# Scores from opposite row halves, five score places and chunks weighed in twos in the last block of an attention

## The reference, cut to what matters

```python
c = jnp.concatenate([mem, kv], axis=1)                       # mem and kv are the same context
qh = (q @ w_q).reshape(B, L, N_HEAD, D_HEAD).transpose(0, 2, 1, 3)
kvp = c @ w_kv
k, v = (kvp[..., :D_HEAD], kvp[..., D_HEAD:])
attn_score = jnp.einsum('bhid,bjd->bhij', qh, k) / np.sqrt(D_HEAD)
attn_prob = jax.nn.softmax(attn_score, axis=-1)
out = jnp.einsum('bhij,bjd->bhid', attn_prob, v)
return out.transpose(0, 2, 1, 3).reshape(B, L, D) @ w_concat
```

## Time and profile before

| | |
|---|---|
| median of 3 runs | 2044.11 us |
| lowest, highest run | 2040.64, 2044.14 us |
| profiled execution, span from first to last instruction | 2039.6 us |
| of it, the last block, first score to copy of its sums | 1214.7 to 1285.3 us |
| mean granted TensorE clock | 0.986 of full |

### The profile page before, as it was taken

How to read it: one execution, slowest core, us unless ns; L and a number is a source line. 1 busy time by engine, 2 the same in 40 slices (tenths; PEclk the granted TensorE clock), 3 DMA queues, 4 the chain that set the end, 5 groups by cost and what they waited for, 6 DMA issues and landing times. The chain is left out here.

```text
span 2039.6 us, 36001 instructions
## 1 busy us (share of the span) xinstructions
PE 1959.2 (96%) x14245; PEld 969.3 (48%) x14245; DVE 1573.2 (77%) x2868; ACT 1355.8 (66%) x2394; POOL 100.9 (5%) x85
## 2 busy tenths in 40 slices
PE   7779999999999999999999999999999998999997
PEld 2225744444444444444444444444344444777755
DVE  7997899999999999999999981233688865444344
ACT  5333488888888888888888887432578874443321
POOL 1661000000000000000000000000200000000000
PEclk8999999999999999999999999999999999999999
DMA  4210000000000000000000000232000000000000
GB/s 148 73 62 0 1 2 2 2 1 2 1 1 2 2 1 2 2 2 1 1 2 1 2 2 1 60 120 65 0 1 1 2 1 0 1 1 1 16 29 28
DMA packets 25043, 32.66 MB, mean 16 GB/s; under 512 B 5967, under 2 KB 20335, under 8 KB 24622
## 3 DMA queue, kind: packets, MB, share of 16 engines
q1 hardware_dynamic: 23694, 28.30, 4.5%
q10 hardware_dynamic: 1184, 2.10, 0.3%
HBM read 29.61 MB, written 0.65 MB: 15 GB/s over the span
## 5 line engine op out<-in xcount | busy, mean ns | idle before, releaser
L1069 DVE TENSOR_REDUCE sb_max_partial<-ps_max_ps 128x1 f32<-128x512 f32 (+1 forms) x1664 | 977.3, 662 | 43.9 <-PE ps_max_ps L836 43.1
L1053 ACT ACTIVATE sb_probs<-ps_score_ps 128x512 f32<-128x512 f32 (+1 forms) x1632 | 875.1, 597 | 117.6 <-PE ps_score_ps L974 71.7
L974 PE MATMUL ps_score_ps<-sb_q_stack,sb_key_stack 64*128 64x512 f32 x1632 | 586.6, 443 | 3.9 <-ACT sb_probs L1053 3.4
L836 PE MATMUL ps_max_ps<-sb_key_stack,sb_q_stack 64*128 64x512 f32 (+1 forms) x1560 | 555.9, 438 | 0.0
L963 PE MATMUL ps_acc_ps<-sb_probs,sb_val_ones 128*32 128x256 f32 x6528 | 465.0, 387 | 0.0
L974 PEld LDWEIGHTS ps_score_ps<-sb_q_stack,sb_key_stack 64*128 64x128 f32 x1632 | 275.8, 183 | 321.5 <-ACT sb_probs L1053 257.2
L836 PEld LDWEIGHTS ps_max_ps<-sb_key_stack,sb_q_stack 64*128 64x128 f32 x1560 | 265.0, 184 | 9.8 <-DVE sb_max_partial L1069 7.5
L963 PEld LDWEIGHTS ps_acc_ps<-sb_probs,sb_val_ones 128*32 128x32 f32 x6528 | 156.3, 108 | 207.7 <-issue 140.5
L1721 DVE TENSOR_REDUCE sb_s_max_partial<-ps_s_ps 128x1 f32<-128x512 f32 x256 | 158.5, 682 | 24.6 <-PE ps_s_ps L1567 24.5
L1708 ACT ACTIVATE sb_s_probs<-ps_s_ps 128x512 f32<-128x512 f32 x256 | 140.8, 597 | 30.8 <-PE ps_s_ps L1595 22.8
L1942 DVE TENSOR_SCALAR_CACHE_REDUCE sb_x_scores<-ps_x_score_ps 128x1024 f32<-128x1024 f32 (+1 forms) x56 | 62.0, 1110 | 69.2 <-PE ps_x_score_ps L1929 69.2
(11 more groups left out here) (299 smaller groups left out, 1802.7 us busy)
## 6 DMA issues: line engine op xcount, KB each, us to landing
sb_val<-c_rows SPq DMA_DIRECT2D x16, 512.0 KB, 3.6
sb_e_gate_rows<-e_gate_dram SPq DMA_DIRECT2D x15, 512.0 KB, 3.9
sb_e_w<-L_ffn_rW SPq DMA_DIRECT2D x30, 128.0 KB, 2.1
sb_e_w<-L_ffn_W_T SPq DMA_DIRECT2D x24, 128.0 KB, 2.1
sb_ctx_T<-ctx_T SPq DMA_DIRECT2D x1, 1664.0 KB, 7.6
sb_ctx_T<-ctx_T ACTq DMA_DIRECT2D x1, 1538.0 KB, 8.6
sb_x_T<-x_T SPq DMA_DIRECT2D x1, 512.0 KB, 3.8
sb_x_tok<-x ACTq DMA_DIRECT2D x1, 512.0 KB, 11.0
```

The costliest lines, as they stand in the source:

```text
L836: nc.tensor.matmul(bank((blk, u))[:, 0:n], queries, keys, start=True, stop=True).then_inc(tile_ready, 1)
L974: nc.tensor.matmul(score_ps[:, e % 3, :], k.key_stack[rows(blk), c * P:(c + 1) * P], q_stack[rows(blk), blk // 2, j * HALF:(j + 1) * HALF] ...
L1053: nc.scalar.activation(probs[0:n, c % 3, j * HALF:(j + 1) * HALF], score_ps[0:n, e % 3, :], ACT.Exp).then_inc(exp_done, 1)
L1069: nc.vector.tensor_reduce(partial[:, blk % 2, h, r:r + 1], bank((blk, u))[:, 0:RANGES[r][1]], AX.X, ALU.max).then_inc(tile_used, 1)
```

## The change

Only the last block's order and places change, and one copy is added in block 1:

- The second score of each chunk (odd e) reads keys from rows 0 to 63 and queries from rows 0 to 63 of `q_first`, instead of rows 64 to 127 of the stacks. So the two scores of a chunk use opposite halves of the array's rows.
- For this, ACT copies the second half of block 15's queries (64 x 512) from `q_stack` to `q_first`, in block 1 behind chunk 12 (`lower_queries`). The shift rows of that half are later moved to `q_first` instead of `q_stack`.
- The last block's scores use five PSUM places: the three of `score_ps` and places 2 and 3 of `max_ps`. A score waits for the exponential five before it.
- Its chunks are weighed two at a time, after scores 7, 11, 15, ... 99, two and three chunks behind; chunks 48, 49 and 50 are weighed after the last score.

```diff
--- before.py
+++ after.py
@@ -777,7 +777,7 @@
 
 
 
-            TURN_AT, LAST_AT, FIRST_TURN = 28, NCH - 1, 66
+            TURN_AT, LAST_AT, FIRST_TURN, LOWERED_AT = 28, NCH - 1, 66, 12
             first = [(0, u) for u in range(FIRST_TURN + 1)] + [(0, "A")] + [(0, u) for u in range(FIRST_TURN + 1, TILES)]
 
 
@@ -858,7 +858,16 @@
                 eng.wait_ge(shift_turned, 2 * blk + (1 if half == "A" else 2))
                 lo = HALF_P * (blk % 2) + TERMS
                 cols = slice(0, HALF) if half == "A" else slice(HALF, BLK)
-                copy(q_stack[lo:lo + 2, blk // 2, cols], bank((blk, half))[0:2, :]).then_inc(shift_ready[half], 1)
+                if blk == NB - 1 and half == "B":
+                    to = q_first[TERMS:TERMS + 2, cols]
+                else:
+                    to = q_stack[lo:lo + 2, blk // 2, cols]
+                copy(to, bank((blk, half))[0:2, :]).then_inc(shift_ready[half], 1)
+
+            def lower_queries(act):
+
+                act.wait_ge(tile_used, TILES)
+                nc.scalar.copy(q_first[0:HALF_P, HALF:BLK], q_stack[rows(NB - 1), NT - 1, HALF:BLK].bitcast(F32))
 
             def q_bank(i):
 
@@ -964,16 +973,30 @@
                                            probs[:, v % 3, q * QUART:(q + 1) * QUART], start=(v == 0), stop=(v == NCH - 1))
                 ins.then_inc(pv_done, 1)
 
+            LAST_BANKS = 5
+
+            def score_bank(blk, e):
+                if blk < NB - 1:
+                    return score_ps[:, e % 3, :]
+                i = e % LAST_BANKS
+                return score_ps[:, i, :] if i < 3 else max_ps[:, i - 1, :]
+
             def score(pe, blk, e):
 
                 c, j = divmod(e, JOBS)
                 if c == 0:
                     pe.wait_ge(shift_ready["AB"[j]], blk + 1)
-                if not (blk == 0 and e < 3):
-                    pe.wait_ge(exp_done, blk * EXPS + e - 2)
-                nc.tensor.matmul(score_ps[:, e % 3, :], k.key_stack[rows(blk), c * P:(c + 1) * P],
-                                 q_stack[rows(blk), blk // 2, j * HALF:(j + 1) * HALF], start=True,
-                                 stop=True).then_inc(score_ready, 1)
+                if blk < NB - 1 or e < 3:
+                    if not (blk == 0 and e < 3):
+                        pe.wait_ge(exp_done, blk * EXPS + e - 2)
+                elif e >= LAST_BANKS:
+                    pe.wait_ge(exp_done, blk * EXPS + e - LAST_BANKS + 1)
+                if blk == NB - 1 and j == 1:
+                    keys, queries = k.key_stack[0:HALF_P, c * P:(c + 1) * P], q_first[0:HALF_P, HALF:BLK]
+                else:
+                    keys = k.key_stack[rows(blk), c * P:(c + 1) * P]
+                    queries = q_stack[rows(blk), blk // 2, j * HALF:(j + 1) * HALF]
+                nc.tensor.matmul(score_bank(blk, e), keys, queries, start=True, stop=True).then_inc(score_ready, 1)
 
             def fin(t, step):
                 return len(FINISH) * t + FINISH.index(step) + 1
@@ -1023,6 +1046,10 @@
                     of = e // 6 * 3
                     if e == 0 and blk > 0:
                         weigh(pe, blk - 1, NCH - 1)
+                    elif blk == NB - 1:
+                        if e % 4 == 3 and e > 4:
+                            weigh(pe, blk, e // JOBS - 3)
+                            weigh(pe, blk, e // JOBS - 2)
                     elif e % 6 == 2 and of > 0:
                         weigh(pe, blk, of - 2)
                         weigh(pe, blk, of - 1)
@@ -1034,6 +1061,8 @@
                         turn_back(pe, BACK_AT[e])
                     if blk == NB - 1 and e in PROJECTED_AT:
                         project(pe, PROJECTED_AT[e])
+                if blk == NB - 1:
+                    weigh(pe, blk, NCH - 3)
                 weigh(pe, blk, NCH - 2)
                 if blk + 1 < NB:
                     issue(pe, (blk + 1, "B"))
@@ -1050,10 +1079,12 @@
                     for j in range(JOBS):
                         e = c * JOBS + j
                         act.wait_ge(score_ready, blk * EXPS + e + 1)
-                        nc.scalar.activation(probs[0:n, c % 3, j * HALF:(j + 1) * HALF], score_ps[0:n, e % 3, :],
+                        nc.scalar.activation(probs[0:n, c % 3, j * HALF:(j + 1) * HALF], score_bank(blk, e)[0:n, :],
                                              ACT.Exp).then_inc(exp_done, 1)
                         if e == 0 and blk > 0:
                             take_acc(act, blk - 1)
+                    if blk == 1 and c == LOWERED_AT:
+                        lower_queries(act)
                     if c == TURN_AT and blk + 1 < NB:
                         take_shift(act, nc.scalar.copy, blk + 1, "A")
                     if blk * NCH + c in job_at:
```

## The result

The changed kernel took 2031.6 us, median of 4 runs (2030.5 to 2032.7), against 2043.8 for the kernel before on the same chip: a ratio of 0.9941, 95% interval 0.9927 to 0.9956, 12 us faster. In a second trial it was 2033.0 against 2041.0, 0.9957 (0.9944 to 0.9970), 8 us faster. Forecast were 2034.2 and a range of 2028 to 2040.

A forecast was written before the change was run, and what follows sets the result against it. PE, working strictly in order, was taken to bound the last block; its step prices put the last exponential 10.2 us earlier, less 0.3 for the copy: 9.9 off the 2044.1 median, so 2034.2 us, range 2028 to 2040.

The forecast's parts named there:

- PE's sum: Last block: PE's in-order step prices add up to its length, 68.9 us predicted for the old order against 68.6 measured.
- the ring: Last block's three probability slots: costed at nothing, 0.1 a group if uncovered; as rival, splitting weighings too, 5.5 us lost, 10%.
- Opposite halves: Last block's scores: a chunk's two scores cost one slot, so two chunks' four scores take 0.66 us instead of 1.12.
- Weighing in twos and the finishing steps: Last block: 1.00 us per two chunks; transposes, turn back and project 8.8, plus 0.20 or 0.43 per break, 15.2 in all.
- Five places: Last block's scores: score e waits for exponential e - 5, scores 3 and 4 for nothing; no separate gain given.
- The copy: Half the queries copied on ACT in block 1: costs between 0 and 0.6 us, taken as 0.3.
- the step from span to median: Whole run: profiled span 2039.6 us against median 2044.1, so a forecast span of 2029.7 became 2034.2.
- ACT as the bound: Rival, last block: exponentials 0.49 us apart set the limit, 18.7 us saved, 2025.7 us; 10%.
- No overlap: Rival, last block: opposite halves do not overlap, a group takes 2.12 us, 2.4 us saved, 2042.0 us; 6%.
- a drain at each change of half: Rival, last block: every score costs 0.43 us, a group 2.72, last exponential 7.8 us later, 2052.2 us; 4%.
- The sign named for it: Sign of the ring in the last block: PE's loads of scores or weighings released by ACT in nearly every group.

The follow-up runs named there:

- the third experiment: Changed kernel with three score places in the last block, the two of `max_ps` unused for scores: last block 72.11 us against 58.27, run time 2046.7 and 2046.9 us.

## Why the prediction was right

*PE's sum* was the right account. The forecast had score 100 at 1272.2 and the last exponential at 1273.4; it was at 1273.96, and 0.31 of that is that the block began later in this execution (1215.68 for 1215.37). What is left, 0.25, is the ring: costed at nothing, but 0.12 long in the two groups that have no finishing step to cover it (1.78 for 1.66), as the text had bounded it at 0.1 a group. Of the 23 groups, 20 took their price to 0.02 us; the third that did not, the turn back of the fourth tile, took 1.97 for 1.92, as turn backs do in the kernel with the steps behind the weighings. One term was put together wrongly: 1217.29 + 0.43 + 1.00 gives score 8 at 1218.72 and not 1218.78. The sum left out the 0.05 between the end of an exponential and the score that waits for it, and the 0.06 too much came to nearly the same; that was luck.

*Opposite halves:* a pair is one slot, as a score and a tile of maxima were the earlier trace rows. That these were different products did not matter.

*Weighing in twos and the finishing steps:* 1.00 a group, and breaks at 0.20 and 0.43, show in the groups to 0.02 us, and the experiment that removes all breaks gives back 5.4 of the 6.4 us costed for them; most of the rest is PE's wait for a place in the nine lightest groups, not a smaller price.

*Five places:* the forecast treated them as a condition met and did not say what they are worth. By the third experiment they are what makes the rest possible: 13.8 us.

*The copy:* taken at 0.3 between 0 and 0.6, it shows no price. It stood in a block where ACT has room, and the lower bound was the right end: block 2 began 127.66 us after block 0, where it had been 127.62.

*The time:* 9.9 us were forecast off the span, and 9.6 came off it. The median came out 2.6 us under the 2034.2 named, because the step from span to median was taken as 4.5 us from one profile, while the changed kernel's median lay 1.6 over its own. Every run whose span is on record took 1.7 to 1.8 us more than that span; the other 2.8 of the 4.5 are, by that, the distance of the one profiled execution from the median, and carry nothing of the change. So how near the median came is chance; how near the block came is not.

*The rivals.* ACT as the bound (10%) did not come, for the reason given: nearly every group carries a finishing step. Without the broken pairs PE begins to wait for ACT, in the lightest groups: 1.97 where PE needs 1.92. The Trainium skill, TensorEngine Tiling (Array Packing), PSUM Bottleneck, says that emptying PSUM may become the bottleneck once tiling has sped up TensorE; the trace agrees in these groups alone. No overlap and a drain at each change of half are excluded by the common start at 1229.72 and by the 7.5 us that the block loses with one half of the rows. The ring was to cost 0.1 in each group and to split the weighings: a double weighing took 1.00 (1224.09 - 1223.09) and not 1.14, and 20 groups took their price. The sign named for it, loads put down to ACT, does appear in 17 places, but the exponentials named had mostly long ended.

## What to carry to other kernels

Where one engine runs a written-out order without gaps, price each step by the distance between the starts of neighbouring steps, try the prices on the stage as it stands, and only then on the new order; here they hold to 0.3 us of 58. Other work put between the scores cost, beside its own time, a new first slot for the scores behind it: 0.20 between two pairs and 0.43 inside one. So it belongs where such a switch stands anyway, not between two products that overlap. When steps are sent in larger lots, count the buffers around the ring: the same order lost 3.9 us with three places and won 10 with five.

## What the runs showed of the hardware

PE's busy share says nothing of such a gain. Three kernels' windows table within the last block, the one before, the changed one and the one with the steps behind the weighings (the window's length, then PE busy):

```profile
1216.00:1284.00 68.00, 67.78 (x550) 31.52 (x548) 10.44 (x42) 54.71 (x102) 0.00 (x0) 1.00 0.01 1
```

```profile
1220.50:1278.50 58.00, 57.78 (x550) 27.25 (x550) 10.43 (x42) 52.10 (x103) 0.00 (x0) 1.00 0.01 2
```

```profile
1216.00:1269.00 53.00, 52.77 (x554) 25.81 (x550) 10.44 (x42) 51.35 (x103) 0.00 (x0) 1.00 0.01 2
```

PE is busy 99.6 or 99.7% of each, for some 550 matmuls in 68, 58 and 53 us alike. And the mean recorded length of an exponential is not the same in all kernels: 597 ns before, 600 with three places, 607 changed and 619 to 621 with the steps behind the weighings, though exponentials in a row start 0.48 to 0.49 apart in each; why was not tried.
